# RWKV block, one core: read-out by token halves in two PSUM banks, and the first state folded in at token 64

## The reference

```
def step(s, rkvw):
    r_t, k_t, v_t, w_t = rkvw
    a = k_t[:, :, :, None] * v_t[:, :, None, :]
    out = jnp.einsum('bhk,bhkd->bhd', r_t, u * a + s)
    return (a + w_t[:, :, :, None] * s, out)
...
_, outs = jax.lax.scan(step, s0, xs)
```

## Time and profile before

| | us |
|---|---|
| median of 3 runs | 1711.39 |
| lowest and highest | 1710.81, 1713.77 |
| the profiled execution, device time | 1713.96 |
| its span, first to last instruction | 1712.2 |

### The profile page before, as it was taken

One profiled execution on the slowest core, in us unless ns is written; L12 is line 12 of the kernel. 1 busy time (PEld: TensorE's weight loads), 2 busy tenths in 40 slices (PEclk: granted clock), 3 DMA queues, 4 the chain that ended last, 5 costly groups with the idle time before them and its releaser, 6 DMA issues.

```text
span 1712.2 us, 41121 instructions
## 1 busy us (share of the span) xinstructions
PE 1594.7 (93%) x17600; PEld 1188.1 (69%) x17600; DVE 965.3 (56%) x1942; ACT 553.3 (32%) x898; POOL 644.2 (38%) x540
## 2 busy tenths in 40 slices
PE   4869799999999999999999999999999999999865
PEld 3658577777767677777767777776777777675533
DVE  3263665657666565766566566656656576645312
ACT  1122332334232333434233333433223342333221
POOL 3142432525353352535244253524325252523210
PEclk8889899999999999999999999999999999999888
DMA  7000100101010010101010110101001010100100
GB/s 262 1 26 16 42 13 26 42 16 51 13 55 13 28 39 28 39 15 55 13 38 27 30 40 14 54 13 53 13 26 42 19 48 13 42 13 26 37 25 13
DMA packets 65333, 59.04 MB, mean 34 GB/s; under 512 B 24256, under 2 KB 57408, under 8 KB 64128
## 3 DMA queue, kind: packets, MB, share of 16 engines
q1 hardware_dynamic: 65152, 56.41, 10.6%
HBM read 35.36 MB, written 8.39 MB: 26 GB/s over the span
## 4 chain that ended last, share of the span: by engine, by line
PE 75%; DVE 14%; ACT 4%; issue 3%; POOL 2%; SPq 1%; DMA 1%; POOLq 0%; ACTq 0%; DVEq 0%
PE pair L896 27%; PE pair L904 19%; PE pair L950 5%; PE at_ps L839 4%; PE at_ps L832 3%; PE att_ps L887 3%; PE pair L974 2%; PE pair L930 2%; DVE x L573 2%; PE att_ps L859 2%; DVE kT L486 2%; PE pair L912 2%; PE pair L976 2%; POOL cen L402 2%; PE att_ps L878 1%
## 5 line engine op out<-in xcount | busy, mean ns | idle before, releaser
L896 PE MATMUL pair<-x,wts 128*128 128x256 f32 x2048 | 463.5, 385 | 9.0 <-ACT kT L702 7.6
L896 PEld LDWEIGHTS pair<-x,wts 128*128 128x128 f32 x2048 | 387.9, 192 | 73.2 <-ACT kT L702 12.0
L376 POOL TENSOR_TENSOR x<-x,xnT 128x1024 f32<-128x1024 f32 x80 | 178.5, 2231 | 266.8 <-DVE x L573 266.0
L573 DVE SCALAR_TENSOR_TENSOR x<-pair,vecs,sx 128x256 f32<-128x256 f32 x320 | 132.5, 476 | 191.6 <-PE pair L950 191.6
L713 ACT ACTIVATE at<-at_ps 64x512 f32<-64x512 f32 x256 | 151.1, 590 | 224.1 <-PE at_ps L839 222.3
L904 PE MATMUL pair<-wts,yT 128*128 128x512 f32 x256 | 120.8, 617 | 4.5 <-POOL yT L414 4.5
L896 PE MATMUL pair<-yT,wts 128*128 128x256 f32 x512 | 118.0, 390 | 5.2 <-DVE yT L657 5.2
L904 PE MATMUL pair<-wts,cen 128*128 128x512 f32 x256 | 116.5, 599 | 0.0
L904 PE MATMUL pair<-wts,sx 128*128 128x512 f32 x256 | 114.1, 599 | 1.3 <-ACT cen L697 1.1
L896 PEld LDWEIGHTS pair<-yT,wts 128*128 128x128 f32 x512 | 98.5, 195 | 21.9 <-issue 8.8
L456 DVE SCALAR_TENSOR_TENSOR bonv<-rT,vecs,kT 128x128 f32<-128x128 f32 x128 | 39.0, 367 | 128.2 <-ACT rT L702 78.6
(11 more groups left out here) (134 smaller groups left out, 2602.0 us busy)
## 6 DMA issues: line engine op xcount, KB each, us to landing
rm<-rst SPq DMA_DIRECT2D x1024, 12.0 KB, 1.8
xu<-in_x SPq DMA_DIRECT2D x16, 512.0 KB, 3.8
wts<-in_wts SPq DMA_DIRECT2D x8, 1024.0 KB, 13.4
s<-in_s SPq DMA_DIRECT2D x128, 64.0 KB, 1.8
x<-in_x SPq DMA_DIRECT2D x16, 512.0 KB, 4.4
out<-sx SPq DMA_DIRECT2D x16, 512.0 KB, 3.2
prev<-in_prev SPq DMA_DIRECT2D x32, 4.0 KB, 4.0
maa<-in_maa SPq DMA_DIRECT2D x1, 448.0 KB, 3.8
```

What stands on the lines that cost most here:

```text
L376: gp.tensor_tensor(t, t, xnT[:, :, :, 1:L1].rearrange("p g b t -> p (g b) t"), ALU.add).then_inc(x5_ready, 1)
L573: last = ve.scalar_tensor_tensor(seqs(x5[q], g), ps[:, :, g * L:(g + 1) * L], vecs[:, vec, g:g + 1], seqs(sx, g), ALU.add, ALU.mult)
L896: last = pe.matmul(ps[:, g // 2, TB * (g % 2):TB * (g % 2 + 1)], wts[:, m, k, g * P:(g + 1) * P], source[:, k, :], start=(k == 0), stop=(k ...
```

## The change

**Read-out.** V(n) now treats the two 64-token halves apart. att_ps is one tensor over two banks, one for each half c, with both sequences in each. s0 is multiplied with 64 tokens only (L889), kvs with the other 64 (L891), and each of the eight products of `at` becomes two, with 64 rows of v and `at` and 64 columns (L900). `at` and at_ps keep 64 columns for a head; at_ps is one bank now, not two, and E(n) one instruction.

**First state.** The effect of s0 on the second half goes through kvs: behind the mask (L617) VectorE adds `s0 * du` for each g, four scalar_tensor_tensor of 128x128 (L624). GpSimd's product for tokens 64 to 127 (L363) falls away, and rst has 320 columns for a group instead of 384. s0 is loaded for four units at once (S0, S1 in SP_ORDER) instead of unit by unit, and a mask copy now waits for A(n-2) instead of V(n-2).

**A bank for kt, kv and aT.** They share kv_ps, which brings new waits in turn_k and turn_att.

**Order.** See the lists: wv.0 and A0 go ahead of kt0, and kv0 behind wv.1; aT0 goes behind r.1; on VectorE wv goes ahead of kv0 and c1v_0 ahead of chain0b; on GpSimd bon0 ahead of rch0b.

```diff
-PE_ORDER = ["mixW", "V7", "kt0", "wv.0", "aT1", "kv0", "A0", "wv.1", "z", "V0", "mixK", "c02_1", "A1", "mixG",
+PE_ORDER = ["mixW", "V7", "wv.0", "aT1", "A0", "kt0", "wv.1", "kv0", "z", "V0", "mixK", "c02_1", "A1", "mixG",
...
-            "kt1", "wo.1", "aT0", "kv1", "mixV", "A4", "r.0", "r.1", "V4", "x2T", "A5", "v.0", "v.1", "xT",
+            "kt1", "wo.1", "kv1", "mixV", "A4", "r.0", "r.1", "aT0", "V4", "x2T", "A5", "v.0", "v.1", "xT",
...
-SP_ORDER = ["x", "M1", "M2", "out", "x2", "M3", "M4", "M5", "M6", "M7", "M0"]
+SP_ORDER = ["x", "M1", "S0", "M2", "out", "x2", "M3", "M4", "M5", "S1", "M6", "M7", "M0"]
...
-        at_ps = [ctx.enter_context(nc.psum_tensor(f"at_ps{q}", [P, 512], F32)) for q in range(2)]
-        att_ps = [ctx.enter_context(nc.psum_tensor(f"att_ps{b}", [P, E], F32)) for b in range(NB)]
+        at_ps = ctx.enter_context(nc.psum_tensor("at_ps", [P, 512], F32))
+        att_ps = ctx.enter_context(nc.psum_tensor("att_ps", [P, 2, NB, G, 64], F32))
+        kv_ps = ctx.enter_context(nc.psum_tensor("kv_ps", [P, E], F32))
...
                 if blk.past(UNITS, n - 1):
-                    sp.wait_ge(read_done, blk.count(UNITS, n - 1))
-                sp.dma_start(s0[p][:, :], A["s0"][blk.index(), n]).then_inc(s0_in[p], 16)
+                    sp.wait_ge(levels_done, blk.count(UNITS, n - 1))
...
-                gp.tensor_tensor(rst[:, b, :, R128B:RST], rst[:, b, :, R64B:R16C],
-                                 carryover[:, :, 0, 4:5].broadcast_to([P, G, 64]), ALU.mult)\
-                  .then_inc(rchain, 1)
...
                     ve.tensor_tensor(kvs[:, :].rearrange("p (g c) -> p g c", g=G),
-                                     att_ps[b][:, :].rearrange("p (g c) -> p g c", g=G),
+                                     kv_ps[:, :].rearrange("p (g c) -> p g c", g=G),
                                      headall[:, :].unsqueeze(1).broadcast_to([P, G, P]), ALU.mult)\
-                      .then_inc(kvs_ready, 1)
+                      .then_inc(kvm_ready, 1)
+                    ve.wait_ge(kvm_ready, a.count(2, b + 1))
+                    ve.wait_ge(s0_in, a.count(32, 16 * (b + 1)))
+                    for g in range(G):
+                        last = ve.scalar_tensor_tensor(kvs[:, g * P:(g + 1) * P], s0[:, g, :],
+                                                       du[:, 2 * g, 4:5], kvs[:, g * P:(g + 1) * P],
+                                                       ALU.mult, ALU.add)
+                    last.then_inc(kvs_ready, 1)
...
-                for c in range(2):
-                    rows_ = slice(64 * c, 64 * c + 64)
-                    last = ac.activation(at[rows_, :, rows_],
-                                         at_ps[n % 2][rows_, :].rearrange("p (h t) -> p h t", h=HG), ACT.Copy)
-                last.then_inc(at_ready, 1)
+                ac.activation(at[:, :, :], at_ps[:, :].rearrange("p (h t) -> p h t", h=HG), ACT.Copy)\
+                  .then_inc(at_ready, 1)
...
-                if at_.past(2, b - 1):
-                    pe.wait_ge(att_ready, at_.count(2, b - 1))
+                if b == 0 and at_.past(2, 0):
+                    pe.wait_ge(att_ready, at_.count(2, 0))
+                if b == 1:
+                    pe.wait_ge(kvs_ready, at_.count(2, 1))
...
                 pe.wait_ge(attT_ready, at_.count(2, b + 1))
+                pe.wait_ge(kvs_ready, at_.count(2, 2))
+                if b == 1:
+                    pe.wait_ge(att_ready, at_.count(2, 1))
...
-                pe.matmul(o[:, g * P:(g + 1) * P], s0[n % 2][:, :], rst[:, b, g, R64A:RST],
-                          start=(g == 0), stop=False, skip_group_check=True)
-                pe.matmul(o[:, g * P + 64:(g + 1) * P], kvs[:, g * P:(g + 1) * P], rst[:, b, g, R64B:R16C],
-                          start=False, stop=False, skip_group_check=True)
+                pe.matmul(o[:, 0, :], s0[:, g, :], rst[:, b, g, R64A:RST], start=(g == 0), stop=False,
+                          skip_group_check=True)
+                pe.matmul(o[:, 1, :], kvs[:, g * P:(g + 1) * P], rst[:, b, g, R64B:R16C], start=(g == 0),
+                          stop=False, skip_group_check=True)
...
-                        last = pe.matmul(o[32 * quad:32 * quad + 32, g * P:(g + 1) * P],
-                                         vtm[b][:, first:first + 32], at[:, h, :], start=False,
-                                         stop=(g == G - 1), skip_group_check=True)
+                        for c in range(2):
+                            rows_ = slice(64 * c, 64 * c + 64)
+                            last = pe.matmul(o[32 * quad:32 * quad + 32, c, :],
+                                             vtm[b][rows_, first:first + 32], at[rows_, h, :], start=False,
+                                             stop=(g == G - 1), skip_group_check=True)
```

More of the change, by code:

```diff
@@ L55 @@
     "kt0": 0, "kt1": 0, "kv0": 0, "kv1": 0, "attb1": -1, "attb0": 0, "aT1": -1, "aT0": 0}
-PE_ORDER = ["mixW", "V7", "kt0", "wv.0", "aT1", "kv0", "A0", "wv.1", "z", "V0", "mixK", "c02_1", "A1", "mixG",
+PE_ORDER = ["mixW", "V7", "wv.0", "aT1", "A0", "kt0", "wv.1", "kv0", "z", "V0", "mixK", "c02_1", "A1", "mixG",
             "V1", "decay", "A2", "k.0", "k.1", "yT", "V2", "g.0", "g.1", "c1v_1", "A3", "mixR", "wo.0", "V3",
[1 row of a table removed]
[1 row of a table added]
             "V5", "c02_0", "A6", "kk.0", "kk.1", "c1v_0", "V6", "rr.0", "rr.1", "h", "A7"]
-ACT_ORDER = ["kt0", "att1", "E0", "gn_square", "z", "gn_std", "E1", "decay", "E2", "k", "yT", "g", "vtm1",
+ACT_ORDER = ["att1", "E0", "kt0", "gn_square", "z", "gn_std", "E1", "decay", "E2", "k", "yT", "g", "vtm1",
              "E3", "kt1", "E4", "r", "x2T", "E5", "v", "xT", "E6", "att0", "kk", "vtm0", "rr", "h", "E7"]
-DVE_ORDER = ["mixW", "attb1", "chain1", "gn_sum", "kv0", "wv", "gn_var", "mixK", "c02_1", "gn_rec", "mixG",
+DVE_ORDER = ["mixW", "attb1", "chain1", "gn_sum", "wv", "kv0", "gn_var", "mixK", "c02_1", "gn_rec", "mixG",
              "chain1b", "ln1_stats", "ln1", "g", "c1v_1", "mixR", "attb0", "wo", "ln2_stats", "kv1", "mixV",
-             "ln2", "chain0", "x2T", "c02_0", "xT", "chain0b", "c1v_0"]
+             "ln2", "chain0", "x2T", "c02_0", "xT", "c1v_0", "chain0b"]
 POOL_ORDER = ["mixW", "gn_sub", "rch1", "wv", "mixK", "gn_scale", "mixG", "c02_1", "rch1b", "ln1_stats",
-              "yT", "bon1", "mixR", "ln2_stats", "mixV", "rch0", "c02_0", "rch0b", "bon0"]
-SP_ORDER = ["x", "M1", "M2", "out", "x2", "M3", "M4", "M5", "M6", "M7", "M0"]
+              "yT", "bon1", "mixR", "ln2_stats", "mixV", "rch0", "c02_0", "bon0", "rch0b"]
+SP_ORDER = ["x", "M1", "S0", "M2", "out", "x2", "M3", "M4", "M5", "S1", "M6", "M7", "M0"]
 class Block:
@@ L147, in build @@
         rm = [sb(f"rm{p}", [P, HG, RMW]) for p in range(2)]
-        s0 = [sb(f"s0{q}", [P, P]) for q in range(2)]
-        at = sb("at", [P, HG, L])
+        s0 = sb("s0", [P, G, P])
+        at = sb("at", [P, HG, 64])
         vtm = [sb(f"vtm{b}", [P, 2 * E]) for b in range(NB)]
@@ L185, in build @@
         wts_in = [sem(f"wts_in{m}") for m in range(8)]
-        s0_in = [sem(f"s0_in{q}") for q in range(2)]
+        s0_in, kvm_ready = sem("s0_in"), sem("kvm_ready")
         rm_in = [sem(f"rm_in{p}") for p in range(2)]
@@ L433, in _ @@
             ve.memset(du[:, :, 0], 1.0).then_inc(setup, 1)
-            for q in range(2):
-                ve.memset(at_ps[q][:, :], 0.0).then_inc(setup, 1)
-            ve.memset(at[:, :, :], 0.0).then_inc(setup, 1)
+            ve.memset(at_ps[:, :], 0.0).then_inc(setup, 1)
             ve.memset(k64[:, :], 0.0).then_inc(setup, 1)
@@ L819, in levels @@
                 pe.wait_ge(rm_in[p], at_.count(16 * HG * UNITS // 2, 16 * HG * (n // 2 + 1)))
[L820 to L822 removed]
+                if at_.past(UNITS, n):
+                    pe.wait_ge(at_ready, at_.count(UNITS, n))
+                out = at_ps[:, :].rearrange("p (h t) -> p h t", h=HG)
                 r4, r16 = R4C - R16C, 0
@@ L858, in outer @@
                     v = bass.AP(vtm[b], g * 2 * P, [[2 * E, 64], [64, G], [48, 2], [1, S]])
-                    last = pe.matmul(att_ps[b][:, g * P:(g + 1) * P], kvs[0:64, g * P:(g + 1) * P], v,
+                    last = pe.matmul(kv_ps[:, g * P:(g + 1) * P], kvs[0:64, g * P:(g + 1) * P], v,
                                      start=True, stop=True)
```

45 lines of the change are left out of this document (24 added, 21 removed).

## The result

The changed kernel takes 1788.49 us (median of 4 runs, 1787.54 to 1789.79), the kernel before 1711.1 (4 runs, 1708.58 to 1713.77): a ratio of 1.0453, 95% interval 1.0434 to 1.0471. It is 4.5% slower; the forecast was 1776, in a range of 1738 to 1804. The profiled execution took 1787.59, with a span of 1785.8. Ratios leave out runs that are over 1.5% above the fastest of their kernel, which touches e5 alone: two of its ten, whose median of 1724.3 is 1718 without them.

A forecast was written before the change was run, and what follows sets the result against it. TensorE's own work was taken as the bound, VectorE's chain for the second sequence close behind. Thirteen steps of +4.8 us (62), start-up +3 and last step 0 made +65 on the 1711.39 median: 1776, range 1738 to 1804.

The forecast's parts named there:

- The hold: VectorE's four folds behind kv0's mask are held by GpSimd's queue, so V0 waits a new 4.3 us a step.
- The hand-over: VectorE beside GpSimd: with GpSimd's next operation ready, one VectorE operation gets through between two of GpSimd's.
- The other signs: In kv0, folds' mean about 1 us with one over 2; L420's start unchanged; clock near 0.96; V4 0.86.
- rival A: Folds on VectorE aren't held, or get through together: V0 at Z+3.2, step -1.1, 1692 us; chance 0.13.
- The clock: From V0 to mixG, slow clock behind the new wait costs 2.5 us a step, ends 0 and 3.2.
- Rival B: V0's wait comes without clock loss, 1744; or last fold slips ahead of L420, clock lost, about 1743; chance 0.20.
- The read-out: Each V unit on TensorE 0.20 us shorter: 0.10 from the state product, 0.10 from the products of at.
- Rival D: A read-out longer than before; chance 0.02.
- The rest of the step: Behind mixG: 0.5 us less of L486's 2.40; behind g.0, V3 to V6 save 0.8.
- What costs nothing: One at_ps bank, kt0, aT0 behind r.1, later chain0b: no cost; S0 should land 2 us before the fold.
- The ends: First two steps: folds add some 2 and 3 us, less 2 of savings, +3; last step 0.
- Z: Moment in a step when wv.1 ends and z starts on TensorE; the prediction counts V0 and mixG from it.

The follow-up runs named there:

- e5: Changed kernel with the fold split into product and sum, the s0 product ahead of wv on VectorE: 1724.3 us, ratio 1.0034 to the kernel before.
- e6: Changed kernel with GpSimd's wv moved behind its mixK: 1763.9 us, ratio 1.0311 to the kernel before.
- e4: Changed kernel with the fold as two VectorE operations of 128x512 (product, then sum) in place of four of 128x128: 1739.9 us (one run).
- e11: Changed kernel with the mask written back into kv_ps and the four folds reading it from PSUM: 1708.4 us, ratio 0.9994 to the kernel before.
- e2: Changed kernel with four unused 128x512 products put in front of V0, inside the wait: 1740.5 us, ratio 1.0178 to the kernel before.
- e9: e5 with the copy of s0 issued ahead of the mask copies M1: 1689.7 us, ratio 0.9876 to the kernel before.
- e7: Changed kernel with each read-out's 16 products written all for the first token half, then all for the second: 1791.4 us (one run).
- e1: Changed kernel without the folds, with GpSimd's product and a third state product of 64 columns again: 1704.9 us, ratio 0.9968 to the kernel before.
- e3: Changed kernel with V0 moved behind mixK and c02_1 on TensorE: 1715.5 us, ratio 1.0032 to the kernel before.

## Why the prediction was right, and where it was off

- **The hold, and its size.** Forecast: a new wait of 4.3 us, 13 times, since one fold gets through at each end of a GpSimd operation. Measured: 13 times 4.2. The prediction had the folds through at 2.15, 3.0, 3.9 and 6.3 us behind the end of wv.1; they end at 2.3, 3.1, 4.0 and 6.3 behind the start of kv0 (921.23). The hand-over rested on one operation (L456); e6, e4 and e11 show it from three sides: the queue shortened, the fold in fewer pieces, and the operand moved to PSUM. The other signs came too: the four folds of kv0 have a mean of 1.15 us with one of 2.42, and GpSimd's wv starts 3.8 us behind wv.1 where it had been 3.7. That the engines wait for each other through semaphores only, as the section on the chip says, doesn't hold for VectorE and GpSimd: the last fold took 2.42 beside GpSimd's L423 of 2.39, where all four took 1.12 in e11.
- **Who waits for whom.** e4 shows both orders: the sum (903.09 for 1.11) waits for GpSimd's L337 (902.46 for 1.19), and L343 for the sum (1.15, where it took 0.83 in the changed kernel). Which of the two comes first is decided anew for each instruction: the first fold ends behind gn_sub (923.55 and 923.38), and each of the three behind it has to wait for an operation more. So rival A, the folds not held, fell: 4.34 us for the four.
- **The clock, the term that failed.** From the stretch at 0.50 behind the wait of 2.16 us the cost was put at 2.5 us a step, on the guess that some of the slow time would lie inside the wait; 0 and 3.2 were the ends. No run shows the 2.5. e2 measures 3.4, above the upper end, and even above the 2.9 read from the first step of the start-up. V0 to mixG takes 8.6 at 0.52 to 0.62 against 5.14 at 1.00 (e9). The missing 0.9 times 13 is 12 us. Rival B, no fall of the clock, is e2's time: 1740.5, where it said 1744.
- **The read-out.** Forecast 0.86 for V4, measured 0.88. The split was off, and the sum came out right by luck. The two state products were to gain 0.10 and gained nothing: the first takes 0.17 in place of 0.22, but that with kvs 0.32 in place of 0.27. The products of `at` were to gain 0.10 and gained 0.18 (0.39 in place of 0.57 until the next work); that the overlap of the row halves is the reason isn't shown (e7). That e1 gave up 0.22 for a third product of 64 columns, as much as the first product of the kernel before took with 128, says that the number of state products matters more than their columns. Rival D, a read-out longer than before, fell with V4's 0.88.
- **The rest of the step.** g.0 to the next z was put at 76.8 and took 76.82. mixG to g.0 was to gain 0.5 and gained 0.6, but by other terms than the prediction's, which wanted 0.5 of L486's 2.40. That operation, now L487, fell to 0.42, and L484 ahead of it from 0.90 to 0.28; the copy behind it went from 0.89 to 2.22, held by the same GpSimd addition, and a later product (L495) from 0.28 to 0.94. The hold moved down the chain instead of going away. The zt wait is gone, as said; the k wait came to 3.4 us in 13 steps, less than the 0.5 to 0.9 a step that was expected and less than the 5.8 before.
- **What costs nothing.** One at_ps bank, kt0 behind A0, aT0 behind r.1 and the later chain0b show no wait in the middle; g.0 to z leaves no room for one. s0's copy was on time for the folds in the middle, as said; that it had little room shows in e5, which wanted it 2.5 us sooner.
- **The ends.** Forecast +3, all in the start-up, where the folds were to make the two waits of V0 longer by 2 and 3 us. That failed: they fell from 2.16 and 2.68 to 1.36 and 1.83, z to V0 stayed at 3.3 and 3.8, and the middle begins 0.5 us earlier than before. The last block, put at 0, cost 0.5. So the ends give nothing, and 13 times 5.7 is the whole of the 73.6 us between the two profiled executions (spans 1712.2 and 1785.8). The medians lie 77.4 apart; the other 3.8 are scatter: the profiled execution of the kernel before is 2.9 above the median of its runs, that of the changed one 0.9 below. The miss of 12 us is therefore 12 too little for the clock, 3 too much for the start-up and some 4 of scatter: that the clock's 12 alone would fill it is chance.
- **A slip in rival A.** With V0 at Z+3.2 its own terms put mixG 0.4 later and not 0.2, so the time would be some 2 us above its 1692. Nothing hangs on that.

## What to carry to other kernels

When an operation is added to VectorE, look at where its operands live and what GpSimd has queued beside it: here a fold with two SBUF operands took up to the length of the GpSimd operation beside it (2.42 and 2.39; all four 4.34 for work of 1.12), and with one operand in PSUM the same folds weren't held (1.12). Count a wait of TensorE together with what comes behind it: here to 4.2 us of waiting came 3.4 at a granted clock of 0.52 to 0.62. The cure was not to undo the change but to give the folds a PSUM operand and TensorE 1.1 us of work that needn't wait.

## What the runs showed of the chip

- A short wait can cost more than itself. Behind 0.97 us (e11) V0 to mixG was 1.6 longer in 9 of 12 steps (granted clock 0.75) and not at all in 3 (1.00); behind 1.7 (e4) 1.6 (0.75) or 3.2 (0.59); behind 2.1 (e6) 3.1 in most steps (0.59); behind 4.2 between 2.9 and 4.0, alternating (0.62 and 0.52). Behind 0.93 in e3, where mixK and c02_1 stood between z and V0, and behind 0.6 in e9, it cost nothing (1.00), nor did 1.38 in one step of e5 (1.00). So the length of the wait alone doesn't decide; what does is open.
- The same four instructions took 4.34, 2.26 or 1.12 us, by GpSimd's queue and by the home of one operand. A copy with a single SBUF operand took 0.36 or 2.22 (L490).
- A copy that came 0.64 us late cost 8.5 us in that step (e5), since the late product met one GpSimd operation and the sum behind it another.
